# Count matrix of a graph network: 50 ranges of 50 destinations, one chunk a turn from a ring of four slots, in place of 40 ranges of 64 in threes

## The reference

```python
src = randint(40000, 0, 2500)
dst = (2500 * uniform(40000) ** 2).astype(int32)     # skewed to small numbers
order = argsort(dst); src, dst = src[order], dst[order]
x = x + gat2(relu(layernorm(x)), src, dst)           # two attention layers, 8 heads
x = x + relu(layernorm(x)) @ W                       # W = zeros(256, 256).at[src, dst].set(edge_weight)
x = x + sage_and_decoder(relu(layernorm(x)), src, dst)
x = x + gat4(relu(layernorm(x)), src, dst)
```

## Time and profile before

| | before |
|---|---|
| time, median of 3 runs | 2122.45 us (2120.99 to 2123.28) |
| profiled execution | 2122.24 us, span 2120.4 us |
| TensorE busy | 1728.6 us (82%) |
| VectorE busy | 1583.0 us (75%) |
| ScalarE busy | 1378.7 us (65%) |
| GpSimd busy | 303.5 us (14%) |
| matmuls into acc | 1161 (387 chunks x 3) |

### The profile page before, as it was taken

How to read it: one execution, slowest core, us unless ns; L and a number is a source line. 1 busy time by engine, 2 the same in 40 slices (tenths; PEclk the granted TensorE clock), 3 DMA queues, 4 the chain that set the end, 5 groups by cost and what they waited for, 6 DMA issues and landing times. The chain is left out here.

```text
span 2120.4 us, 63580 instructions
## 1 busy us (share of the span) xinstructions
PE 1728.6 (82%) x21987; PEld 1375.2 (65%) x21987; DVE 1583.0 (75%) x3455; ACT 1378.7 (65%) x2350; POOL 303.5 (14%) x451
## 2 busy tenths in 40 slices
PE   4999985598998737899893699998989985488884
PEld 1333333588888627888883477775548984488883
DVE  7989987899999888999999522222332257899996
ACT  0246885999999659999995622221113354799986
POOL 2466511456500020000000000000000001100000
PEclk9999997799999878999997899999999998699997
DMA  2000000010101000010101200000001010000002
GB/s 84 5 1 2 3 2 27 14 40 28 40 27 40 2 27 30 28 40 27 40 27 50 90 8 0 0 0 7 1 20 36 20 61 14 8 21 28 21 22 99
DMA packets 34799, 54.96 MB, mean 26 GB/s; under 512 B 10668, under 2 KB 26240, under 8 KB 34432
## 3 DMA queue, kind: packets, MB, share of 16 engines
q1 hardware_dynamic: 31232, 51.64, 7.2%
q0 software_dynamic: 3328, 0.06, 0.1%
HBM read 43.19 MB, written 8.49 MB: 24 GB/s over the span
## 5 line engine op out<-in xcount | busy, mean ns | idle before, releaser
L1201 PE MATMUL ps<-R,M 128*128 128x132 f16 (+1 forms) x8640 | 827.1, 222 | 189.7 <-DVE M L1120 112.0
L1201 PEld LDWEIGHTS ps<-R,M 128*128 128x128 f16 x8640 | 763.0, 97 | 218.8 <-issue 115.0
L1075 ACT ACTIVATE Rm<-rows,cB 128x1280 bf16<-128x1280 f32 (+3 forms) x816 | 846.9, 1132 | 31.7 <-DVE Mn L1110 18.4
L1209 PE MATMUL ps<-HB,C 128*128 128x66 f16 x6400 | 590.2, 193 | 0.0
L1209 PEld LDWEIGHTS ps<-HB,C 128*128 128x128 f16 x6400 | 571.6, 97 | 0.0
L1120 DVE TENSOR_TENSOR M<-Rm,C 128x1280 f16<-128x1280 bf16 (+3 forms) x816 | 530.7, 674 | 36.9 <-ACT Rm L1075 29.4
L600 PE MATMUL acc<-ohc,ohl 128*128 128x420 f16 (+1 forms) x1161 | 246.3, 349 | 26.3 <-DVE ohl L564 23.6
L562 DVE TENSOR_SCALAR ohc<-cells,near 128x1280 f16<-128x1280 f16 x387 | 214.3, 554 | 27.9 <-PE acc L600 23.4
L1123 DVE SCALAR_TENSOR_TENSOR M<-rows,cN,C 128x1280 f16<-128x1280 f32 (+1 forms) x144 | 217.3, 1509 | 0.0
L600 PEld LDWEIGHTS acc<-ohc,ohl 128*128 128x128 f16 x1161 | 89.8, 98 | 174.9 <-DVE ohl L564 119.4
L1547 PE MATMUL psA<-R,C 128*128 128x512 f16 (+1 forms) x800 | 144.7, 331 | 9.6 <-DVEq L2036 3.7
(11 more groups left out here) (296 smaller groups left out, 2404.3 us busy)
## 6 DMA issues: line engine op xcount, KB each, us to landing
rows<-rowd SPq DMA_DIRECT2D x32, 640.0 KB, 4.0
rows<-rowd SPq DMA_DIRECT2D x16, 320.0 KB, 3.4
xd<-R SPq DMA_DIRECT2D x4, 640.0 KB, 2.9
xr<-xd SPq DMA_DIRECT2D x20, 128.0 KB, 2.1
xd<-HB SPq DMA_DIRECT2D x1, 2560.0 KB, 8.1
xr<-xd SPq DMA_DIRECT2D x5, 512.0 KB, 6.0
R<-in_x SPq DMA_DIRECT2D x1, 2432.0 KB
xr<-in_x SPq DMA_DIRECT2D x19, 128.0 KB, 2.0
```

What stands on the lines that cost most here:

```text
L1075: a.activation(Rm[:, s % SG, 0:wide(p)], rows[:, p % 2, 0:wide(p)], ACT.Relu, bias=cB[:, ds(h + s * nh, 1)]).then_inc(s_R, 1)
L1201: m = pe.matmul(region(p % 2, r), lhsT, rhs, start=first, stop=True, skip_group_check=True)
L1209: m = pe.matmul(both[:, :, cw:2 * cw], C[:, s * NP + p * W + r * P:][:, 0:P], VP[:, s, :, ds(h * cw, cw)], start=False, stop=True, skip_gr ...
```

## The change

The count matrix is built in 50 ranges of 50 destinations (1000 cells) instead of 40 of 64 (1280 cells), in two matmuls of 500 columns a chunk instead of three of 420 and 440. Each range takes exactly its chunks, at least three, and a turn of the loop handles one chunk. The slots are a ring of four, and the slot number is the running number of the chunk modulo four, so the places of `ohc` and `ohl` are now worked out in registers. Searches go one or two to a range in the first 21 ranges, 28 in all, instead of one in each of 40. The columns of C behind destination 2499, which no range covers now, are filled with zeros in the set-up.

```diff
-WW = 64
-NW = NP // WW
-U3 = 3
+WW = 50
+NW = N // WW
+RING = 4
+SEARCHED = [2] * 7 + [1] * 14
+NS = sum(SEARCHED)
...
-        DSPLIT = [(0, 22), (22, 43), (43, 64)]
+        DSPLIT = [(0, 25), (25, 50)]
...
+                g.memset(C[:, :].rearrange("p (s d) -> p s d", d=NP)[:, :, N:NP], 0.0).then_inc(s_xz, 1)
...
-                ch(v.tensor_scalar(threes, threes, 1 / U3, 1 / U3, ALU.mult, ALU.add))
...
+                ch(v.tensor_scalar(counts, counts, 3.0, None, ALU.max))
...
+            def searched(q):
+
+                return range(sum(SEARCHED[:q]), sum(SEARCHED[:q + 1]))
...
+            def slot_of(eng, step):
+
+                return nc.s_assert_within(step % RING, 0, RING - 1, skip_runtime_bounds_check_because="a remainder")
...
-                for q in range(NW):
+                for q in range(NS):
                     w = q % 2
                     with sp.Fori(0, turns) as i:
...
-                    with v.Fori(0, threes) as i:
-                        for u in range(U3):
-                            k = chunk(first + i * U3 + u, NG * P - 1)
-                            v.wait_ge(s_used, (before + i) * U3 + u + 1)
-                            v.tensor_scalar(ohc[:, u, :], cells[:, :], near[:, q % 2, ds(k, 1)], None,
-                                            ALU.is_equal).then_inc(s_oh, 1)
-                            v.tensor_scalar(ohl[:, u, :], lows[:, :], bT[:, ds(k, 1)], None,
-                                            ALU.is_equal).then_inc(s_oh, 1)
-                    before = v.snap(v.to_reg(before + threes), min_val=0, max_val=NW * NCH)
+                    with v.Fori(0, count) as i:
+                        k = chunk(first + i, NG * P - 1)
+                        u = slot_of(v, before + i)
+                        v.wait_ge(s_used, before + i + 1)
+                        v.tensor_scalar(ohc[:, ds(u * CELLS, CELLS)], cells[:, :], near[:, q % 2, ds(k, 1)], None,
+                                        ALU.is_equal).then_inc(s_oh, 1)
+                        v.tensor_scalar(ohl[:, ds(u * P, P)], lows[:, :], bT[:, ds(k, 1)], None,
+                                        ALU.is_equal).then_inc(s_oh, 1)
+                    before = v.snap(v.to_reg(before + count), min_val=0, max_val=NW * NCH)
...
+                    def one(i, opening):
+                        u = slot_of(pe, before + i)
+                        pe.wait_ge(s_oh, (before + i) * 2 + 2)
+                        for b, (d0, d1) in enumerate(DSPLIT):
+                            if opening:
+                                pe.wait_ge(s_out, q * NB + b + 1)
+                            ins = pe.matmul(bank(b, q % 2), ohl[:, ds(u * P, P)], ohc[:, ds(u * CELLS + d0 * NT, (d1 - d0) * NT)],
+                                            start=opening, stop=True, skip_group_check=True)
+                        ins.then_inc(s_used, 1)
+
+                    one(0, True)
+                    one(1, False)
+                    for c in searched(q):
+                        search(c)
+                    with pe.Fori(2, count) as i:
+                        one(i, False)
```

More of the change, by code:

```diff
@@ L339, in _ @@
                 ch.wait()
-                first, threes = row[:, 0, :], row[:, 1, :]
+                first, counts = row[:, 0, :], row[:, 1, :]
                 ch(v.tensor_scalar(first, lh[:, 0, :], -1.0, FAR, ALU.mult, ALU.add))
@@ L477, in first_of, with count_of @@
                                           "the table is built with its first chunk limited to NCH - 1")
-            def threes_of(entry):
-                return nc.s_assert_within(entry // PACK, 2, NCH, skip_runtime_bounds_check_because=
-                                          "the table is built with at least two threes, and no more than cover NCH chunks")
+            def count_of(entry):
+                return nc.s_assert_within(entry // PACK, 3, NCH, skip_runtime_bounds_check_because=
+                                          "the table is built with at least three chunks, and no more than NCH")
+            def slot_of(eng, step):
+                return nc.s_assert_within(step % RING, 0, RING - 1, skip_runtime_bounds_check_because="a remainder")
             @block.gpsimd
@@ L587, in _, with search @@
                 coming, before = packed(pe, 0), 0
+                def search(c):
+                    with pe.Fori(0, turns) as i:
+                        n = turns * c + i
+                        pe.wait_ge(s_sq, n + 1)
+                        hold(pe, s_row[c % 2], turns * (c // 2 * 48) + i * 48 + 48)
+                        pe.matmul(psD[c % 2][:, :], big16[:, :], notlater[:, :, :].rearrange("p u j -> p (u j)"),
+                                  start=True, stop=False)
+                        pe.matmul(psD[c % 2][:, :], left[:, c % 2, :], right[:, c % 2, :], start=False,
+                                  stop=True).then_inc(s_D, 1)
@@ L604, in _ @@
-                    three(0, True)
-                    with pe.Fori(0, turns) as i:
-                        n = turns * q + i
-                        pe.wait_ge(s_sq, n + 1)
-                        hold(pe, s_row[q % 2], turns * (q // 2 * 48) + i * 48 + 48)
-                        pe.matmul(psD[q % 2][:, :], big16[:, :], notlater[:, :, :].rearrange("p u j -> p (u j)"),
-                                  start=True, stop=False)
-                        pe.matmul(psD[q % 2][:, :], left[:, q % 2, :], right[:, q % 2, :], start=False,
-                                  stop=True).then_inc(s_D, 1)
```

71 lines of the change are left out of this document (30 added, 41 removed).

## The result

| | before | after |
|---|---|---|
| time, median | 2121.72 us (2118.68 to 2123.28, 4 runs) | 2257.16 us (2256.97 to 2257.58, 4 runs) |
| ratio | | 1.0642, interval 1.0625 to 1.0659 |
| profiled execution's span | 2120.4 us | 2255.1 us |
| first ohc to last ohc starts | 32.8 to 309.3, 276.5 us | 33.4 to 446.1, 412.7 us |
| next stage's first memset on GpSimd starts | 354.2 us | 488.0 us |

The change costs 135 us, 6.4%. The forecast was 2275 us, range 2215 to 2322. All of the loss lies in the stage that was changed: the next stage begins 133.8 us later, and the whole span is 134.7 us longer.

What follows compares the result with a forecast made beforehand. VectorE was taken to set the stage's pace, after the change through its instruction stream. Turns 398, changes of range 25 and paired searches 7 make 430 us against 277: +153 us, so 2275 us, range 2215 to 2322.

Steps and rivals of the forecast that it cites:

- The mechanism: VectorE's queue in the changed stage: a one-chunk turn's instruction stream outlasts its 0.555 us of engine work and sets the pace.
- The turn: VectorE's loop: one turn's stream takes 1.10 us, bounds 0.95 to 1.20; 362 turns make 398 us.
- The second remainder: Address group of ohc on VectorE: slot number and first chunk each need one; the extra costs 0.08 us, bounds 0 to 0.16.
- The second group: VectorE's queue: one more register group ahead of ohc in each turn, taken as 0.13 us.
- Changes of range: VectorE's stream between ranges: 49 changes, each 0.50 us more than a turn within a range, 25 us in all.
- Pairs of searches: First seven ranges, two searches each: VectorE waits for slots 1 us per pair, 7 us in all.
- TensorE's blocked time: TensorE's queue at two searches in a row: blocked about 4 us in all, late row fetch for the second included.
- four whole turns of cover: Ring of four slots at two searches in a row: four slots at 1.10 us cover all but 1 us of TensorE's delay.
- ScalarE's share: ScalarE's part of the searches: beside the path, as it is busy for only 162 of 281 us.
- Rival 1: VectorE's loop: register work hides behind ohc, pace 0.555 us, stage 242 us, 2087 us in all; chance 0.07.
- Rival 3: VectorE's loop: a turn costs only 0.90 us, stage 361 us, +84, 2206 us in all; chance 0.10.
- Rival 2: TensorE's loop: its stream is slower than VectorE's, 1.15 us a turn, stage 471 us, 2316 us in all; chance 0.09.

Runs made afterwards that it cites:

- the hoisted kernel: Against the changed kernel, VectorE works out a range's first chunk and count once per range instead of in every turn: 2237.05 us, ratio 1.0538.
- rows early: Against the changed kernel, SP may fetch the next search's rows before the matmul of the search before is done: 2246.66 us, ratio 1.0582.
- the ring of 64: Against the kernel before, 40 ranges of 64 and 40 single searches kept, but one chunk a turn from a ring of four slots: 2251.57 us, ratio 1.0607.
- 28 searches: Against the kernel before, only the searches changed: 28 in the first 28 ranges instead of 40; 2116.93 us, ratio 0.9979.
- width 56: Against the kernel before, 45 ranges of 56 and 28 single searches, still three chunks a turn in fixed slots: 2114.42 us, ratio 0.9963.
- fewer cells: Against the changed kernel, ohc compares only the first 600 of 1000 cells, the rest zeroed once, counts incomplete: 2261.09 us, ratio 1.0651.
- threes: Against the changed kernel, the old loop of three chunks a turn in fixed slots put back, 50 ranges and paired searches kept: 2157.78 us, ratio 1.0164.
- threes with single searches: Against the changed kernel, three chunks a turn in fixed slots and the 28 searches one to a range, 50 ranges kept: 2126.61 us, ratio 1.0016.

## Why the prediction was right, and what it mis-sized

**The mechanism: right.** VectorE's own stream sets the pace once a turn has one chunk. Fewer cells didn't help, fewer register instructions did, and three chunks a turn took 100 us back.

**The turn: 0.08 us too dear.** Forecast 1.10 us, measured 1.02, which is 28 us of 362 turns (370 and not 398 us), the largest error. By the starts in the turn shown above, which took 1.04 us from head to head: from the head to the address group it is 0.11 us, where the turn before the change that I copied took 0.14. The second remainder added 0.05 us (271 ns against 220), where I had put 0.08. The second group moved the ohc by 0.10 us (address group to ohc 0.42 us against 0.27, less the remainder's 0.05), where I had put 0.13. The step from the ohc by ohl's group to the end group went the other way, 0.18 us and not 0.16. No single step was far off: three small terms were each 0.03 us too large and one 0.02 too small, and the turn in the mean is 0.02 us shorter than this one.

The Trainium skill, "Advanced Engine Details and Errata", section Control Flow Timing, puts compare-and-branch at about 108 ns. The trace doesn't agree: here end group to branch takes 0.125 us and branch to head another 0.19 us, 0.32 us in all as in the rows of before. With the page's figure in its place, by estimate, the stage would have been some 50 us shorter than forecast; it was 17 us shorter, and the branch had no part in that.

**Changes of range: right.** 1.53 us from ohc to ohc in the median (1.19 to 1.96), 0.53 us over a turn in the mean, 49 times: 26 us against 25.

**Pairs of searches: too cheap.** Forecast 1 us each, measured 1.8 to 3.1 us, 18 us in the seven ranges and not 7. TensorE's blocked time was right: from the first search's first matmul to the next chunk's it is 3.8 to 4.7 us, 4.2 in the mean against about 4 (40.54 less 35.96 in the rows above), with the wait on the DMA in it (17.1 us in seven, 2.4 each). Two terms failed. From that chunk's first matmul to the ohc that it sets free it is 1.46 us (42.00 less 40.54), where I had put 0.5. And I counted four whole turns of cover, 4.4 us, from the search's start. VectorE had begun the first of the four 0.5 to 1.2 us before it (35.44 against 35.96), so its next ohc was due 3.1 us after the search's start. 4.2 + 1.5 - 3.1 is 2.6 us a pair. The sum itself was off as well: 4 + 0.5 us against 4 x 1.10 us leaves 0.1 us, not the 1 us that I wrote.

**The sum.** 370 + 26 + 18 = 414 us, against 430 forecast and 413.3 us measured from the first ohc to the end of the last ohl. That the forecast came so near is in part luck: the turns were 28 us too dear and the pairs 11 us too cheap.

**What I had at nothing.** The first ohc is 0.6 us later, within the 1 us allowed. At the stage's end there is a gain of 3.0 us that I had missed. I had said that ScalarE's share was beside the path. Before the change its 40th search was on the path at the end: GpSimd's addition waited for it, and the barrier for GpSimd. After the change the barrier waits for VectorE. So +136.8 us at the last ohc became +133.8 us at the next stage.

**Rival 1, the hidden stream**, gave 2087 us; the ohc would have had to follow every 0.56 us. Refuted. **Rival 3, cheap turns at 0.90 us**, gave 2206 us; the turn lies 0.12 us above it and 0.08 below mine. **Rival 2, TensorE's stream**, doesn't decide here: by the starts of its own instructions a looped turn takes it 0.94 us (0.97 forecast), about 392 us in all by estimate, 20 less than VectorE's. It stands close behind: in the hoisted kernel it is the bound in the first range, at 0.93 and 0.97 us a chunk in turn.

**Open.** The stages behind have the same code in every kernel, yet between the next stage's first memset and the end of the span the profiled executions are longer than before by 0.1 to 1.2 us in some (the change, rows early, the ring of 64, 28 searches, width 56) and by 2.4 to 8.8 us in others (fewer cells 5.4, threes 8.0, threes with single searches 8.8). In threes with single searches over 5 us of it build up in the last 200 us. I have no cause for it; where totals differ by less than that, the stage is what to read. By it, threes with ranges of 50 and single searches are 1.7 us faster than before in the stage, though 4 us slower in all.

## What to carry to other kernels

A loop whose bounds, slots or addresses come from registers costs its engine's stream about 1 us a turn here, whatever the engine does meanwhile, so put enough work in a turn (three chunks, 1.9 us) before making the work itself smaller. How far a stream could run ahead was set here by the semaphore waits that stand in it: count, behind the last slot wait of a range, what the stream must still do before the next range's first instruction. Before you call a helper engine's work hidden, look at which engine the barrier at the stage's end waits for, and don't put two dependent searches (or other round trips) back to back: the pair is as long as its chain, and taking one link away shows the next.

## What the runs showed of the hardware

- A taken branch costs TensorE's stream more than VectorE's: its COMPARE_BRANCH is 215 to 234 ns when taken and 83 ns when not, and the head stands 0.27 to 0.29 us behind its start; on VectorE it is 56 ns when taken and 50 when not, and the head 0.19 us behind.
- On VectorE a register group in a turn takes 211 to 223 ns with one remainder, 271 to 276 ns with two, and 51 to 106 ns with none. TensorE's group with the slot's remainder takes 112 to 120 ns. The starts of short ones stand 0.11 to 0.16 us apart, however short they are.
- At a barrier GpSimd's DRAIN ended 5.3 us after the engine's last instruction, in the kernel before and in the ring of 64 alike, where VectorE's and ScalarE's ended with their last instruction.
- TensorE's granted clock in the stage fell from 1.00 to 0.82 (0.88 from 33 to 300 us, 0.71 from 300 to 440 us) while its matmuls came with gaps between them, and that had no part in the loss: the pace was the same 1.00 us in a range at 1.00, the 2.4 GHz level, and in one at 0.50, the 1.2 GHz level.
- The profile names a releaser for idle time that the stream causes: 110 us of VectorE's idle time were put down to TensorE's matmul, of which 21 us, at the pairs, were that. That the rest was the stream showed only when the engine work was made smaller and nothing else moved.
- In the tenth range of the changed kernel every step from ohc to ohc takes 1.24 to 1.33 us, and in the hoisted kernel 1.16 to 1.22 us in the same range, though its code is that of its neighbours. The instructions are no longer than elsewhere; two gaps between starts are, in the tenth range from the address group to the next one (0.43 us instead of 0.30) and from the branch to the head (0.28 instead of 0.19). The 33rd range (up to 1.54 us) and the 45th (1.23 to 1.26) are slow too. It costs some 3 us in all. The clock isn't it, since the eleventh range has the same 0.50 at 1.00 us a turn, and I have no cause for it.
